# The prologue of a two-layer transformer program: routing by token halves, another order of the loads, Wo summed on TensorE

## The chip, the cores and the metric

One core of one Trainium2 chip runs the whole program. The metric is the device time of one execution in microseconds. TensorE is called PE here, VectorE DVE, ScalarE ACT, GpSimd POOL, and SyncE SP; SP only issues DMA transfers in this program.

## What is computed

2048 tokens of 256 numbers (inputs of shape 2 x 1024 x 256) go through two layers of the form x + s * silu(g), where s is an attention and g a feed-forward part of the same normalized x. The change touches only layer 0:

```python
xn = layernorm(x)
# attention: one K/V head, the values are also the queries of all 16 heads
k, v = xn @ Wk + bk, xn @ Wv + bv
attn = softmax(v @ k.T / 128)                      # per batch
s = concat([attn @ v] * 16) @ Wo + bo              # = (attn @ v) @ sum_over_heads(Wo) + bo
# feed-forward: 64 experts, at most 128 tokens each, hidden size 88
scores = sigmoid(xn @ router_weight.T)
sc = scores + e_bias
# groups of 8 experts, scored by the sum of their two best sc; the 4 best groups stay
masked = where(group in best 4, sc, 0)
topk_idx = top_k(masked, 8)
topk_w = scores[topk_idx] / sum(scores[topk_idx]) * 2.5
# a token's place in an expert = number of earlier tokens that chose it; places over 127 are dropped
moe = scatter_add(silu(x_e @ w_gate[e]) * (x_e @ w_up[e]) @ w_down[e] * topk_w)
g = moe + (silu(xn @ sh_gate) * (xn @ sh_up)) @ sh_down
x = x + s * silu(g)
```

Layer 1 is a grouped attention and a feed-forward part with ternary weights; both kernels compute it by the same code.

## The kernel before

Tokens are in 16 tiles of 128 (NT). Each engine runs a program written out by hand, in order, and semaphores tie them together; there is no scheduler, so the order in the code is the order on the engine. `F` and `A` are two large SBUF areas that several stages use in turn, `two` is the whole of PSUM (eight banks of 128 x 512 float32), W is the area of expert weights and rows.

**Prologue** (to about 85 us). SP loads x in four parts (L311), the router weights and the expert bias (L312, L313), Wk and Wv (L315), their biases (L317), Wo of 2.1 MB (L318) and the weights of the shared expert. DVE takes statistics of x and writes the normalized rows xn (centre, L840). PE waits for the constants and for all six small loads, turns the router weights (L1262), then per tile turns xn into xT (L1279; ACT copies it out of PSUM, L555) and makes the logits of the tile before (L1269, four passes of 64 columns). ACT makes a tanh of them in two halves (L561). K and V follow (L1303, in a buffer of xT's layout `A`), with V turned back to rows (turn_v, L1294). DVE meanwhile routes all 16 tiles at once: scores (L873, L874), the best two of each group by maxima and minima (L877 and on), the four best groups (L892, L896), the masked scores (L899 to L903), the eight best experts (L905, L908), a 0/1 table of experts and tokens (L911) and a running count over it (L912). Then PE turns counts into places (positions, L1338 and L1340), both halves of 32 experts at once, ACT and DVE copy them out (L600, L998), DVE builds the tables by which PE writes each expert's token list (masks L946, hot_high, hot_low, number; slots L1404; spread L982; indices L1413). The normalized weights (L1004 to L1009) are stored beside the rows of xn in DRAM (tok_d, SP, L350). The shared expert is computed between these steps in four groups of 512 tokens: gate and up on PE (shared_up, L1317), tanh on ACT (L587), the product on DVE in two steps (L863, L866), down on PE (L1328), the copy with a factor of 0.25 on ACT (L593). Its rows fill the two DRAM accumulators of the experts' results, acc_d[0] and acc_d[1] (L343; L346 fills rows for tokens that don't exist). POOL writes the constants and adds up Wo over the heads (L428 and L430, 15 additions).

**Expert loop** (64 steps). POOL gathers expert n's rows of tok_d by index (L438), PE turns them (turn, L1432) and makes gate and up (up, L1443), ACT and DVE make the hidden values, PE turns these (turn_h, L1449) and makes down (L1455), DVE scales the rows by the tokens' weights (put, L1023), and POOL scatters them into acc_d[n % 2] with an add (L458). PE's step n is: turn(n+1), up(n), turn_h(n-1), other work, down(n-1). Weights come in groups of two experts in five buffers (load_experts: three transfers a group, L333 and L335). In between stand, by constants: in experts 4 to 7 what is left of the lists of experts 32 to 63 (SLOTS_AT, TURN_AT), and from expert 9 (START) the attention of layer 0 (scores, L1359), whose projection uses WoS, the sum of Wo.

What the names in the change stand for: `rep8`, `gsp`, `gr`, `mx8`, `gmask` are small tables of the group selection; `s_sig`, `s_sc`, `s_masked`, `s_rep` are the scores, biased scores, masked scores and the table with the chosen ones replaced by BIG, all in `F`; `sel16`, `cum16` are the 0/1 table and its count; `then(...)` makes the next DVE instruction wait for this one, `mark(...)` doesn't.

## Time and profile before

| what | value |
|---|---|
| median of three runs | 496.04 us (495.99 to 497.1) |
| the profiled execution | 494.54 us, with a span of 492.7 us |
| mean granted clock of PE over the span | 0.916 |
| busy share over the span | PE 77%, DVE 67%, POOL 64%, PE's weight loads 58%, ACT 46% |
| routing on DVE | 33.50 to 54.6 us |
| first expert's transposes on PE | 85.51 us |
| POOL's eighth scatter (expert 7) | 117.58 us |

The profile is of one execution: the span runs from its first to its last instruction, and its own time holds 1.8 us around that. A share is an average over stages that have different limits, so the table says little by itself; the stages have to be read in time. Starts are counted from the span's start.

### The profile page before, as it was taken

Reading aid. Unit: us, or ns where it says so; the run is one execution under the profiler, and the core shown is the slowest. Engines: PE = TensorE matmul, PEld = TensorE weight load, DVE = VectorE, ACT = ScalarE, POOL = GpSimd, SP = SyncE. Lnnn points to the kernel's source line nnn. Section 1 sums busy time; section 2 is a strip of 40 time slices with the busy share of each in tenths; the row PEclk is TensorE's granted clock in tenths of the full one; section 3 lists DMA queues with packets and bytes.
Section 4 is the critical chain, followed back from the end, with each engine's and each line's share of the span. In section 5 each row is a group of like instructions: output and inputs, shape, how many; then the busy total and the mean of one; then the engine's idle time right before and its main releaser. Section 6 shows DMA issues by size and latency. Waiting matters only on the chain.

```text
span 492.7 us, 7386 instructions
## 1 busy us (share of the span) xinstructions
PE 380.0 (77%) x2246; PEld 286.4 (58%) x2246; DVE 332.1 (67%) x940; ACT 227.7 (46%) x526; POOL 316.9 (64%) x306
## 2 busy tenths in 40 slices
PE   0999868789999878979998973384687857698572
PEld 0974344577776756868886852232365554566562
DVE  6629991855454534646666532859999999999950
ACT  1344323524443436524544423246566656577542
POOL 5440005478887777888888863454787976968872
PEclk9999998799999999979999977589797998889888
DMA  7940056978889997868787546500000000000001
GB/s 251 339 128 0 1 153 220 265 171 196 196 184 226 239 236 172 184 128 204 170 180 171 86 56 195 166 0 0 2 0 23 1 23 1 23 23 11 12 21 43
DMA packets 58872, 57.89 MB, mean 117 GB/s; under 512 B 7099, under 2 KB 56531, under 8 KB 58835
## 3 DMA queue, kind: packets, MB, share of 16 engines
q1 hardware_dynamic: 46547, 38.55, 26.5%
q0 software_dynamic: 12288, 18.88, 20.3%
q8 instruction: 18, 0.29, 0.2%
q14 instruction: 19, 0.16, 0.1%
HBM read 39.69 MB, written 17.73 MB: 117 GB/s over the span
## 4 chain that ended last, share of the span: by engine, by line
DVE 40%; PE 26%; DMA 14%; issue 10%; POOL 4%; ACT 4%; SPq 1%; POOLq 0%; ACTq 0%; DVEq 0%
DMA acc_d<-W,idxE 9%; DVE W L1201 4%; PE two L1395 4%; PE two L1443 4%; DVE nv L1180 3%; DMA W<-tok_d,idxE 3%; PE two L1455 3%; PE two L1359 2%; PE two L1269 2%; DVE nv L1181 2%; DVE W L1204 2%; PE two L1432 2%; DVE W L1023 2%; POOL acc_d L458 2%; PE two L1279 1%
## 5 line engine op out<-in xcount | busy, mean ns | idle before, releaser
L458 POOL DMA_INDIRECT acc_d<-W,idxE x64 | 102.3, 1599 | 28.1 <-issue 13.8
L438 POOL DMA_INDIRECT W<-tok_d,idxE x56 | 56.1, 1002 | 61.6 <-DMA tok_d<-F 44.8
L1046 DVE SCALAR_TENSOR_TENSOR W<-W,two 128x88 f32<-128x88 f32 x64 | 15.6, 244 | 57.8 <-ACT W L678 57.5
L662 ACT ACTIVATE W<-two 128x256 f32<-128x256 f32 x64 | 24.4, 381 | 48.6 <-PE two L1432 48.1
L1543 PE MATMUL two<-wfcT,F 128*128 128x512 f16 x128 | 34.9, 422 | 6.5 <-ACT W L731 6.5
L1395 PE MATMUL two<-A,v 128*128 128x128 f32 x256 | 34.8, 295 | 6.2 <-issue 6.0
L1395 PEld LDWEIGHTS two<-A,v 128*128 128x128 f32 x256 | 33.8, 208 | 8.1 <-issue 7.5
L1023 DVE TENSOR_SCALAR W<-two,W 128x256 f32<-128x256 f32 x56 | 26.8, 479 | 14.7 <-PE two L1455 8.6
L501 POOL TENSOR_TENSOR F<-W,F 128x1024 f16<-128x1024 f32 x16 | 34.1, 2151 | 3.1 <-DVE F L1210 2.6
L1432 PE MATMUL two<-ident,W 128*128 128x128 f32 x112 | 24.3, 300 | 11.4 <-DMA W<-tok_d,idxE 9.2
L1432 PEld LDWEIGHTS two<-ident,W 128*128 128x128 f32 x112 | 19.6, 201 | 22.9 <-DMA W<-tok_d,idxE 13.8
L1443 PE MATMUL two<-W 128*128 128x176 f32 x160 | 32.5, 328 | 0.2 <-ACT W L669 0.2
L1359 PE MATMUL two<-kT,vT 128*128 128x512 f32 x64 | 30.1, 592 | 0.0
L1534 PE MATMUL two<-wqT_hi,F 128*128 128x384 f16 (+1 forms) x64 | 14.4, 329 | 20.2 <-DVE F L1164 20.2
L1583 PE MATMUL two<-wpjT,F 128*128 128x256 f16 x256 | 29.4, 273 | 0.3 <-ACT F L745 0.3
L920 DVE TENSOR_REDUCE nmax<-two 128x1 f32<-128x1024 f32 x16 | 19.6, 1223 | 13.9 <-PE two L1359 13.9
L1583 PEld LDWEIGHTS two<-wpjT,F 128*128 128x128 f16 x256 | 24.9, 98 | 4.3 <-ACT F L745 0.6
L1443 PEld LDWEIGHTS two<-W 128*128 128x128 f32 x160 | 25.9, 204 | 0.7 <-issue 0.7
L1543 PEld LDWEIGHTS two<-wfcT,F 128*128 128x128 f16 x128 | 12.8, 108 | 22.8 <-ACT W L731 8.3
L1455 PE MATMUL two<-W 88*128 88x256 f32 x80 | 24.7, 390 | 1.2 <-DVE W L1023 0.9
L509 POOL TENSOR_TENSOR F<-F 128x256 f32<-128x256 f32 x16 | 11.6, 724 | 21.8 <-DVE F L1217 21.8
L1572 PE MATMUL two<-ident,F 128*128 128x128 f16 x256 | 18.6, 231 | 5.6 <-POOL F L501 3.4
(230 smaller groups left out, 1042.8 us busy)
## 6 DMA issues: line engine op xcount, KB each, us to landing
acc_d<-xn SPq DMA_DIRECT2D x8, 512.0 KB, 4.2
W<-in_L_ffn_w_gate SPq DMA_DIRECT2D x20, 176.0 KB
W<-in_L_ffn_w_up SPq DMA_DIRECT2D x20, 176.0 KB
W<-in_L_ffn_w_down SPq DMA_DIRECT2D x20, 176.0 KB
F<-in_L_ffn_w_gate SPq DMA_DIRECT2D x12, 176.0 KB
F<-in_L_ffn_w_up SPq DMA_DIRECT2D x12, 176.0 KB
F<-in_L_ffn_w_down SPq DMA_DIRECT2D x12, 176.0 KB
x<-in_L_attn_q SPq DMA_DIRECT2D x4, 512.0 KB, 6.0
```

The source lines that it names most:

```text
L438: pool.indirect_dma_start(out=xg[n % XR], out_offset=None, in_=tok_d[:, :], in_offset=bass.IndirectOffsetOnAxis(ap=idxE[:, n:n + 1], axis=0))\
L458: pool.indirect_dma_start(out=acc_d[n % 2][:, :], out_offset=bass.IndirectOffsetOnAxis(ap=idxE[:, n:n + 1], axis=0), in_=ysb[n % YS], in_o ...
L501: pool.tensor_tensor(lo16[n % GT], hid[n // GT % 2][:, n % GT, :], hi16[n % GT], ALU.subtract)\
L662: sc.activation(xgT[n % 2], bk_(2)[:, 0:D].rearrange("p (k n) -> p k n", k=KH), ACT.Copy)\
L1023: ve.tensor_scalar(ysb[n % YS], bk_(3)[:, 0:D], xg[n % XR][:, D + n:D + n + 1], 0.5, ALU.mult, ALU.mult)\
L1359: ins = pe.matmul(two[2][:, 512 * h:512 * h + 512], vT[:, rows], kT[:, at:at + 512], start=True, stop=True)
L1395: ins = pe.matmul(bk_(1)[:, 0:P], v[:, (ORDER[t] // NP) * NP + i, :], probT[t % 2][:, i, :], start=(i == 0), stop=(i == 7))
L1432: ins = pe.transpose(bk_(2)[:, P * k:P * k + P], xg[n % XR][:, 0:D].rearrange("p (n k) -> p k n", k=KH)[:, k, :], ident[:, :])
L1443: ins = pe.matmul(gu[n % 2].rearrange("p (m f) -> p m f", m=2), xgT[n % 2][:, k, :], wgu[r][:, n % WG, :, k, :], start=(k == 0), stop=(k = ...
L1455: pe.matmul(bk_(3)[:, 0:D], hT[n % 2], wdn[(n // WG) % WR][:, n % WG, :], start=True, stop=True)\
L1543: ins = pe.matmul(bk_(2 + h), part[:, n % GT, k, :], wfcT[:, k, 512 * h:512 * h + 512], start=(i == 0), stop=(i == 3))
L1583: ins = pe.matmul(bk_(7)[:, D * (n % GT):D * (n % GT) + D], part[n % 2][:, P * k:P * k + P], wpjT[:, k, :], start=(i == 0), stop=(i == 2 * ...
```

## The change

All of it is in layer 0's prologue and in the first nine experts.

- **Loads and start.** The router weights and the expert bias are first in SP's queue. PE starts with four matmuls on zeros (WARM) whose results nobody reads, then waits for the identity and those two loads alone. DVE makes the zeros, and SP stores them to acc_d[0] and to the rows for tokens that don't exist; only acc_d[1] gets the shared expert's rows, which POOL waits for before expert 1's scatter.
- **Normalizing** is shared: of each four tiles DVE centres two, ACT two (with a bias nmr = -mean * rstd).
- **Routing by halves.** `route(c)` does eight tiles as soon as their logits are there. The sigmoid's factor is folded in (0.5 * tanh + bias + 0.5), groups are masked by a bitwise and, and the scan and the comparison are done for 32 experts at a time (`select(h)`). ACT makes the sigmoid itself from the tanh later.
- **Shared expert.** ACT uses Silu, the product is one DVE step, and the factor of 0.25 is gone. Group 0 of gate and up stands between tile 8 and tile 9 on PE, group 1 ahead of K and V, group 2 after the positions, group 3 after the first indices; down(0) stands between slots and indices, down(2) and down(3) in experts 0 and 1. K and V use two banks instead of four.
- **Wo.** It is loaded into the first half of A, where xT was, once PE has read xT for the last time (`sgu_ps` 4). PE adds it up over the heads by matmuls with the identity, four heads each in experts 3, 6, 7 and 8 (WO_AT); ACT copies the sum in expert 8. POOL's additions are gone.

SP, ahead of the expert loads and after them:

```diff
 ACT_T = 9
+WARM = 4
+WO_AT = (3, 6, 7, 8)
...
         A = sb("A", [P, 8192])
         xT = A[:, 0:4096].rearrange("p (t k n) -> p t k n", t=NT, k=KH)
-        Wo_s = A[:, 4096:8192].rearrange("p (h n) -> p h n", h=HQ)
+        Wo_s = A[:, 0:4096].rearrange("p (h n) -> p h n", h=HQ)
         sh_t = [A[0:FF, 5632 + 512 * i:6144 + 512 * i] for i in range(2)]
-        sh_a = A[0:FF, 6656:7168]
...
         @block.sync
         def _(sp):
+            sp.dma_start(rw_s, rw).then_inc(ld_r, 16)
+            sp.dma_start(eb_b[:, :], eb.rearrange("(a n) -> a n", a=1).to_broadcast([P, NE])).then_inc(ld_r, 16)
             for c in range(4):
                 sp.dma_start(x[:, 4 * c:4 * c + 4, :], x_v[:, 4 * c:4 * c + 4, :]).then_inc(ld_x[c], 16)
-            sp.dma_start(rw_s, rw).then_inc(ld_w0, 16)
-            sp.dma_start(eb_b[:, :], eb.rearrange("(a n) -> a n", a=1).to_broadcast([P, NE])).then_inc(ld_w0, 16)
             for dst, src in ((Wk_s, Wk), (Wv_s, Wv)):
                 sp.dma_start(dst[:, :, :], src.rearrange("(p k) n -> p k n", k=KH)).then_inc(ld_w0, 16)
             for dst, src in ((bkc, bk), (bvc, bv)):
                 sp.dma_start(dst[:, :], src.rearrange("(p a) -> p a", a=1)).then_inc(ld_w0, 16)
-            sp.dma_start(Wo_s, Wo.rearrange("(h p) n -> p h n", p=P)).then_inc(ld_wo, 16)
...
             sp.dma_start(bo_b[:, :], bo.rearrange("(a n) -> a n", a=1).to_broadcast([P, D])).then_inc(ld_sh, 16)
+
+            sp.wait_ge(zeros_ready, 1)
             for c in range(4):
-                sp.wait_ge(xn_ready, 4 * c + 4)
+                sp.dma_start(acc_v[0][:, 4 * c:4 * c + 4, :], zeros.rearrange("p (t d) -> p t d", t=4)).then_inc(acc_zero, 16)
+            for a in acc_d:
+                sp.dma_start(a[NTOK:NTOK + P, :], zeros[:, 0:D]).then_inc(acc_zero, 16)
+            for c in range(4):
+                wait_xn(sp, 4 * c + 1)
+                wait_xn(sp, 4 * c + 3)
                 sp.dma_start(tok_v[:, 4 * c:4 * c + 4, 0:D], xn[:, 4 * c:4 * c + 4, :]).then_inc(xn_stored, 16)
-
-            sp.wait_ge(xn_ready, NT)
...
-                if c == 0:
-                    for a in acc_d:
-                        sp.dma_start(a[NTOK:NTOK + P, :], xn[:, 0, :]).then_inc(acc_init, 16)
-
-            fill_accumulators(0)
             sp.wait_ge(w_ready, 1)
             sp.dma_start(tok_v[:, 0:NT, D:D + NE], s_w).then_inc(w_stored, 16)
             sp.dma_start(tok_d[NTOK:NTOK + P, D:D + NE], s_w[:, 0, :]).then_inc(w_stored, 16)
-            for c in range(1, NT // SC):
-                fill_accumulators(c)
+            for c in range(NT // SC):
+                sp.wait_ge(sy_ready, 2 * c + 2)
+                sp.dma_start(acc_v[1][:, SC * c:SC * c + SC, :], xn[:, SC * c:SC * c + SC, :]).then_inc(acc_shared, 16)
             sp.wait_ge(w_stored, 32)
+            sp.wait_ge(sel_ready, 2)
             for g in range(3, WR):
                 load_experts(g)
+            sp.wait_ge(sgu_ps, 4)
+            sp.dma_start(Wo_s, Wo.rearrange("(h p) n -> p h n", p=P)).then_inc(ld_wo, 16)
             for g in range(WR, NE // WG):
```

POOL, its additions and what it waits for:

```diff
-            pool.wait_ge(ld_wo, 16)
-            then(pool.tensor_tensor(WoS[:, :], Wo_s[:, 0, :], Wo_s[:, 1, :], ALU.add))
-            for h in range(2, HQ):
-                ins = pool.tensor_tensor(WoS[:, :], WoS[:, :], Wo_s[:, h, :], ALU.add)
-                if h < HQ - 1:
-                    then(ins)
-            ins.then_inc(wos_done, 1)
...
-            pool.wait_ge(acc_init, 10 * 16)
+            pool.wait_ge(acc_zero, 6 * 16)
             for n in range(NE):
...
                 pool.wait_ge(y_ready, n + 1)
+                if n == 1:
+                    pool.wait_ge(acc_shared, NT // SC * 16)
```

ACT (the helpers are what the old code did in place, except for `centre` and `sigmoid`):

```diff
+            def centre(c):
+
+                sc.wait_ge(nmr_ready, c + 1)
+                for t in range(4 * c + 2, 4 * c + 4):
+                    sc.activation(xn[:, t, :], x[:, t, :], ACT.Identity, bias=nmr[:, t:t + 1], scale=rstd[:, t:t + 1])\
+                        .then_inc(xn_act, 1)
...
+            def shared_gate(c):
+                sc.wait_ge(sgu_ps, c + 1)
+                if c >= 2:
+                    sc.wait_ge(shT_ready, c - 1)
+                sc.activation(sh_t[c % 2], bk_(shared_bank(c))[0:FF, :], ACT.Silu).then_inc(ssilu_ready, 1)
+
...
+            def sigmoid(c):
+
+                sc.wait_ge(sc_ready, c + 1)
+                sc.activation(s_sig[:, 8 * c:8 * c + 8, :], s_sig[:, 8 * c:8 * c + 8, :], ACT.Copy, bias=0.5, scale=0.5)\
+                    .then_inc(sig_ready, 1)
+
...
             root(0)
             sc.wait_ge(rwT_ps, 1)
             sc.activation(rwT[:, :, :], bk_(4)[:, 0:KH * NE].rearrange("p (k e) -> p k e", k=KH), ACT.Copy).then_inc(rwT_ready, 1)
+            centre(0)
+            take_xT(0)
...
+            take_xT(2)
+            take_xT(3)
+            centre(1)
+            take_xT(4)
+            take_xT(5)
+            root(2)
+            take_xT(6)
+            take_xT(7)
+            centre(2)
+            take_xT(8)
+            root(3)
+            sc.wait_ge(consts, 1)
+            sc.activation(warm[:, :], warm[:, :], ACT.Silu)
+            take_xT(9)
+            take_xT(10)
+            centre(3)
+            take_logits(0)
+            for t in range(11, NT):
+                take_xT(t)
+            take_logits(1)
+            shared_gate(0)
...
+                if n == WO_AT[-1]:
+                    sc.wait_ge(wos_ps, 1)
+                    sc.activation(WoS[:, :], bk_(0)[:, 0:D], ACT.Copy).then_inc(wos_done, 1)
```

DVE:

```diff
+                ve.scalar_tensor_tensor(out=nmr[:, cols], in0=mv[:, cols, 0], scalar=-1.0, in1=rstd[:, cols], op0=ALU.mult,
+                                        op1=ALU.mult).then_inc(nmr_ready, 1)
+                for t in range(4 * c, 4 * c + 2):
                     ve.tensor_scalar(xn[:, t, :], x[:, t, :], mv[:, t, 0:1], rstd[:, t:t + 1], ALU.subtract, ALU.mult)\
-                        .then_inc(xn_ready, 1)
+                        .then_inc(xn_dve, 1)
...
+            ve.wait_ge(ld_r, 2 * 16)
+            then(ve.tensor_scalar(eb_b[:, :], eb_b[:, :], 0.5, None, ALU.add))
             centre(3)
...
 
             def shared_product(c):
-                ve.wait_ge(stanh_ready, c + 1)
-                b = 4 * (c % 2)
-                if c:
-                    ve.wait_ge(shT_ready, c)
-                then(ve.scalar_tensor_tensor(out=sh_a, in0=sh_t[c % 2], scalar=1.0, in1=bk_(b)[0:FF, :], op0=ALU.add, op1=ALU.mult))
+                ve.wait_ge(ssilu_ready, c + 1)
...
+                ve.tensor_tensor(sh_h[c % 2], sh_t[c % 2], bk_(shared_bank(c) + 1)[0:FF, :], ALU.mult).then_inc(shT_ready, 1)
+
+            def route(c):
+
+                ts, gs = slice(8 * c, 8 * c + 8), slice(64 * c, 64 * c + 64)
+                ve.wait_ge(tanh_ready, c + 1)
+                ve.scalar_tensor_tensor(out=s_sc[:, ts, :], in0=s_sig[:, ts, :], scalar=0.5,
+                                        in1=eb_b[:, :].unsqueeze(1).to_broadcast([P, 8, NE]), op0=ALU.mult, op1=ALU.add)\
+                    .then_inc(sc_ready, 1)
+                ve.wait_ge(sc_ready, c + 1)
...
+                then(ve.tensor_scalar(gmask[:, ts, :], gr[:, ts, 0:GROUPS], BIG / 2, -1.0, ALU.is_ge, ALU.mult))
+                then(ve.tensor_tensor(masked_bits[:, gs], sc_bits[:, gs],
+                                      gmask[:, ts, :].rearrange("p t g -> p (t g)").unsqueeze(2)
+                                      .to_broadcast([P, 8 * GROUPS, PER_G]), ALU.bitwise_and))
...
+            def select(h):
+
+                es = slice(HE * h, HE * h + HE)
+                then(ve.tensor_scalar(sel16[:, es, :], s_rep[:, :, es].rearrange("p t e -> p e t"), BIG / 2, None, ALU.is_ge))
+                ve.tensor_tensor_scan(cum16[:, es, :].rearrange("p e t -> p (e t)"), keep16.rearrange("p e t -> p (e t)"),
+                                      sel16[:, es, :].rearrange("p e t -> p (e t)"), 0.0, ALU.mult, ALU.add)\
+                    .then_inc(sel_ready, 1)
+
+            for c in range(2):
+                route(c)
+            select(0)
             shared_product(0)
+            shared_product(1)
...
+            ve.wait_ge(acc_zero, 6 * 16)
             hot_low(0, 0, SB)
             number(0)
 
+            ve.wait_ge(sig_ready, 2)
```

PE:

```diff
-            pe.wait_ge(consts, 1)
-            pe.wait_ge(ld_w0, 6 * 16)
+            pe.wait_ge(zeros_ready, 1)
+            for _ in range(WARM):
+                pe.matmul(bk_(7), zeros[:, 0:P], zeros[:, 0:512], start=True, stop=True)
+            pe.wait_ge(ident_ready, 1)
+            pe.wait_ge(ld_r, 2 * 16)
...
+            def shared_up(c):
+                if c == 0:
+                    pe.wait_ge(ld_sh, 4 * 16)
+                    pe.wait_ge(xT_ready, SC)
+                if c >= 2:
+                    pe.wait_ge(shT_ready, c - 1)
+                for m in range(2):
...
+                if t == NT // 2:
+                    shared_up(0)
...
+            shared_up(1)
+            pe.wait_ge(ld_w0, 4 * 16)
...
+            positions(0)
+            shared_up(2)
             pe.wait_ge(v_ready, 4)
...
+            def sum_wo(i):
+
+                if i == 0:
+                    pe.wait_ge(ld_wo, 16)
+                    pe.wait_ge(sy_ready, NT // 2)
+                for h in range(4 * i, 4 * i + 4):
+                    ins = pe.matmul(bk_(0)[:, 0:D], ident[:, :], Wo_s[:, h, :], start=(h == 0), stop=(h == HQ - 1))
+                if i == 3:
+                    ins.then_inc(wos_ps, 1)
+
             pe.wait_ge(pos_act, 1)
             for g in range(HG):
                 slots(0, g)
+            shared_down(0)
             indices(0)
+            shared_up(3)
+            positions(1)
             shared_down(1)
-            shared_up(3)
-            shared_down(2)
-            shared_down(3)
...
-            pe.wait_ge(sy_ready, NT // 2)
+            pe.wait_ge(sy_ready, 4)
             pe.wait_ge(idxE_ready, 1)
+            pe.wait_ge(pos_act, 2)
...
+                if n < 2:
+                    shared_down(2 + n)
+                if n in WO_AT:
```

**Where instructions stand now.** `two` is PSUM, W and A are the areas above; the words in brackets are the semaphores that an instruction waits for. First PE in expert 3, before:

```order
L1443 MATMUL two<-W 128x176 [waits hT_ready,ld_e1,xgT_ready]
L1443 MATMUL two<-W 128x176
L1449 MATMUL two<-ident,W 88x128 [waits h_ready]
L1455 MATMUL two<-W 128x256 [waits y_ready,hT_ready]
L1432 MATMUL two<-ident,W 128x128 [waits xgT_ready,xg_ld5]
```

and after:

```order
L1525 MATMUL two<-W 128x176 [waits hT_ready,ld_e1,xgT_ready]
L1525 MATMUL two<-W 128x176
L1531 MATMUL two<-ident,W 88x128 [waits h_ready]
L1495 MATMUL two<-A,ident 128x256 [waits sy_ready,ld_wo]
L1495 MATMUL two<-A,ident 128x256 x3
L1537 MATMUL two<-W 128x256 [waits y_ready,hT_ready]
L1514 MATMUL two<-ident,W 128x128 [waits xgT_ready,xg_ld5]
```

Between turning the hidden values of expert 2 and its down matmul, PE now adds up four heads of Wo, and waits there for its load (ld_wo). SP's queue from the routing weights on, before:

```order
L343 DMA acc_d<-xn 128x4x256 [waits sy_ready]
L343 DMA acc_d<-xn 128x4x256
L346 DMA acc_d<-xn 128x256 x2
L350 DMA tok_d<-F 128x16x64 [waits w_ready]
L351 DMA tok_d<-F 128x64
L343 DMA acc_d<-xn 128x4x256 [waits sy_ready]
L343 DMA acc_d<-xn 128x4x256
L343 DMA acc_d<-xn 128x4x256 [waits sy_ready]
L343 DMA acc_d<-xn 128x4x256
L343 DMA acc_d<-xn 128x4x256 [waits sy_ready]
L343 DMA acc_d<-xn 128x4x256
L333 DMA F<-in_L_ffn_w_gate 128x2x176 [waits w_stored]
```

and after:

```order
L366 DMA tok_d<-F 128x16x64 [waits w_ready]
L367 DMA tok_d<-F 128x64
L370 DMA acc_d<-xn 128x4x256 [waits sy_ready] x4
L358 DMA F<-in_L_ffn_w_gate 128x2x176 [waits sel_ready,w_stored]
L358 DMA F<-in_L_ffn_w_up 128x2x176
L360 DMA F<-in_L_ffn_w_down 88x2x256
L358 DMA F<-in_L_ffn_w_gate 128x2x176
L358 DMA F<-in_L_ffn_w_up 128x2x176
L360 DMA F<-in_L_ffn_w_down 88x2x256
L376 DMA A<-in_L_attn_Wo 128x16x256 [waits sgu_ps]
L358 DMA W<-in_L_ffn_w_gate 128x2x176 [waits y_ps]
```

The fills of shared rows now stand behind the store of the weights and go to one accumulator, and Wo's load stands behind these fills and two groups of expert loads. Last, ACT around the logits, before:

```order
L547 ACTIVATE rstd<-rstd 128x4 [waits ln1_var]
L555 ACTIVATE A<-two 128x256 [waits xT_ps] x12
L561 ACT_TABLE_LOAD
L561 ACTIVATE F<-two 128x512 [waits logits_ps] x2
L573 ACTIVATE kT<-two,bks 128x512 [waits kv_ps,bks_ready]
```

and after:

```order
L573 ACTIVATE A<-two 128x256 [waits xT_ps]
L562 ACTIVATE rstd<-rstd 128x4 [waits ln1_var]
L630 ACT_TABLE_LOAD
L630 ACTIVATE warm<-warm 128x1 [waits consts]
L573 ACTIVATE A<-two 128x256 [waits xT_ps] x2
L568 ACTIVATE xn<-x,nmr,rstd 128x256 [waits nmr_ready]
L568 ACTIVATE xn<-x,nmr,rstd 128x256
L578 ACTIVATE F<-two 128x512 [waits logits_ps]
L573 ACTIVATE A<-two 128x256 [waits xT_ps] x5
L578 ACTIVATE F<-two 128x512 [waits logits_ps]
L590 ACTIVATE A<-two 88x512 [waits sgu_ps]
```

The first half's tanh (L578) now stands among the tiles, behind two tiles and two centred rows that come after tile 8, and the table load stands ahead of them.

## Rows read from the trace of the kernel before

**Rows 1.** Page, busy time and shares of the span.
```profile
PE 380.0 (77%) x2246; PEld 286.4 (58%) x2246; DVE 332.1 (67%) x940; ACT 227.7 (46%) x526; POOL 316.9 (64%) x306
```

**Rows 2.** Chain of waits in the prologue: start us, us, what.
```profile
5.83 6.32 DMA bvc<-in_L_attn_bv
...
16.15 0.43 PE two L1279 x2
...
17.32 0.43 PE two L1279 x2
...
33.50 0.70 DVE F L873
```

**Rows 3.** Timeline, weight loads and matmuls: start us, us, engine, line, what [idle before].
```profile
33.01 0.34 PEld L1303 LDWEIGHTS two<-A,F 128*128 128x128 f32 x1 [0.52 <-issue]
...
33.86 0.34 PEld L1303 LDWEIGHTS two<-A,F 128*128 128x128 f32 x1 [0.52 <-issue]
...
34.48 0.19 PEld L1303 LDWEIGHTS two<-A,F 128*128 128x128 f32 x1 [0.28 <-issue]
34.91 0.19 PEld L1303 LDWEIGHTS two<-A,F 128*128 128x128 f32 x1 [0.24 <-issue]
...
50.18 3.64 PE L1317 MATMUL two<-A,sgu 128*88 128x512 f32 x8 [0.78 <-ACT v L566]
```

**Rows 4.** Windows: stretch, length, PE, PEld, DVE, ACT, POOL, PE clock, DMA share, GB/s.
```profile
19.00:20.00 1.00, 1.00 (x8) 1.00 (x7) 1.00 (x2) 0.34 (x1) 0.92 (x2) 1.00 1.09 385
92.00:93.00 1.00, 0.20 (x1) 0.23 (x2) 0.88 (x5) 1.00 (x5) 0.97 (x1) 0.62 1.03 270
297.00:298.00 1.00, 0.91 (x7) 0.45 (x5) 0.00 (x0) 0.85 (x3) 0.00 (x0) 0.98 0.77 84
```

**Rows 5.** Groups by line and form, DVE, prologue: busy us, mean ns, idle before.
```profile
L908 DVE MATCH_REPLACE8 F<-mx,F 128x64 f32<-128x64 f32 x16 | 3.1, 205 | 0.0
L912 DVE TENSOR_TENSOR_SCAN F<-F 128x1024 f16<-128x1024 f16 x1 | 2.3, 2291 | 0.0
...
L874 DVE TENSOR_TENSOR F<-F,eb_b 128x1024 f32<-128x1024 f32 x1 | 1.2, 1226 | 0.0
...
L982 DVE TENSOR_TENSOR F<-two,diag 128x512 f32<-128x512 f32 x1 | 0.7, 692 | 0.0
```

**Rows 6.** Timeline, from the positions to the first expert.
```profile
54.67 0.39 PE L1338 MATMUL two<-F,before 128*128 128x512 f16 x1 [0.85 <-DVE F L912]
...
56.67 0.29 DVE L946 TENSOR_SCALAR F<-F 128x512 int16<-128x512 int16 x1
...
85.51 0.50 PE L1432 MATMUL two<-ident,W 128*128 128x128 f32 x2 [0.69 <-ACT xn L593]
```

**Rows 7.** Timeline, POOL: first gather, second and eighth scatter.
```profile
74.92 1.20 POOL L438 DMA_INDIRECT W<-tok_d,idxE  x1 [44.84 <-DMA tok_d<-F]
...
97.26 1.59 POOL L458 DMA_INDIRECT acc_d<-W,idxE  x1 [0.30 <-issue]
...
117.58 1.59 POOL L458 DMA_INDIRECT acc_d<-W,idxE  x1 [0.30 <-DVE W L1023]
```

**Rows 8.** Timeline, SP's queue issues, and POOL's first reader of Wo.
```profile
6.46 0.60 SPq L318 DMA_DIRECT2D A<-in_L_attn_Wo  x1
...
18.10 0.72 POOL L428 TENSOR_TENSOR WoS<-A 128x256 f32<-128x256 f32 x1 [7.30 <-DMA A<-in_L_attn_Wo]
...
95.74 0.37 SPq L333 DMA_DIRECT2D W<-in_L_ffn_w_gate  x1
...
96.69 0.42 SPq L335 DMA_DIRECT2D W<-in_L_ffn_w_down  x1
```

**Rows 9.** Timeline, PE and DVE in experts 3 to 9.
```profile
94.65 1.06 PE L1455 MATMUL two<-W 88*128 88x256 f32 x2
...
109.85 1.88 PE L1359 MATMUL two<-kT,vT 128*128 128x512 f32 x4
...
115.11 0.48 DVE L1023 TENSOR_SCALAR W<-two,F 128x256 f32<-128x256 f32 x1
```

270 lines of the change are left out of this document (128 added, 142 removed).

## The prediction

> **What bounds the kernel now.** I read the page's shares first: no engine is full over the whole span (PE 77%, DVE 67%, POOL 64%) [rows 1], so the bound has to be read by stage. The expert loop is paced by POOL: scatters start 3.19 us apart (97.26 to 117.58 holds the second to the eighth, one longer step among them; the scatter's own issue takes 1.59 of a step, a gather's issue and the gaps the rest) [rows 7]. What starts the loop later starts all that follows later, and POOL has almost nothing to catch up with. So the change is worth what it moves the eighth scatter (expert 7, 117.58), the first one by which all changed work is done. Ahead of the loop I read the chain of waits, then each engine's timeline: PE waits for the last bias until 12.15, then turns tiles and makes logits; DVE routes from 33.50 [rows 2] until PE takes the positions at 54.67 [rows 6]; slots, indices and the shared expert follow, and the first expert's transposes start at 85.51 [rows 6].
>
> **PE's start, clock and logits.** PE no longer waits for six small loads but for two, router weights and bias, which are first in the queue. The x loads start 1.24 us later for it (two small issues). Two sets of statistics, the reciprocal and two rows lie between x and the first rows: about 10.0 instead of 12.7. Then the clock decides. Before, one tile (two transposes, four logits passes) takes 1.17 us (16.15 to 17.32, and so for the tiles after it), and a transpose 0.21 of it (two take 0.43) [rows 2]; these are times of the lower level, since in the later, dense K/V work a half matmul goes from 0.85 us (33.01 to 33.86) to 0.43 (34.48 to 34.91) [rows 3]. The granted clock shows 1.00 there only because its first change is not yet recorded. The four warm-up matmuls are eight halves of 0.85, 6.8 us at most, done by 8.5. They may raise the clock. After them PE has 1.5 to 3 us of nearly nothing, then tiles that come as DVE delivers them, at about half use. In the loop the clock fell within 92 to 93, where PE worked 0.20 us of one [rows 4]. So I take the lower level again from about the third tile: tile 8 at 18.5, its predecessor's logits at 19.7.
>
> Here speaks a row against me: at 297 the clock rose to 0.98 while PE did nothing but transposes [rows 4]. If transposes keep it up as well as they raise it, the logits stage could run at the upper level; that is the second rival. The Trainium skill ("TensorE: Matmul & The Clock Gate", Part 4, PE-mode transpose) says the opposite, that transposes do not count as activity for the gate. By it the stage would stay low, as I forecast; the row contradicts it as a reason.
>
> **Shared gate matmuls in the middle.** The first group (eight halves, 3.64 us at the upper level [rows 3]) now stands between tile 8 and tile 9. Starting low it costs between 3.4 (it rises at once) and 6.9 (never); in the K/V work it rose near 34.3 [rows 3], some way in, so I take the middle, 5.1: 24.8. ACT turns to the first half's tanh only after two more tiles and two rows that it now centres, all behind that group: 27.7. The new table load for Silu stands where ACT waits for PE, and the one for Exp ahead of a wait: both nothing, 1.3 each if uncovered.
>
> **Routing by halves.** The chain before is 21.1 us from 33.50 to 54.6 [rows 2, 6]. A half has eight of each per-tile instruction (16 replaces at 0.205 [rows 5]), and half-wide elementwise ones: 0.69 instead of 1.23 [rows 5]. One TENSOR_SCALAR of 0.70 and the one for sigmoid go. I get 9.3 per half, 18.7 for both, and half of the compare and the scan (2.29 [rows 5]), 1.8. From 27.7 that is 48.2, 6.4 earlier. But PE stands behind it: from 24.8, seven tiles at 0.6 plus ACT's tanh (30.9), the second gate group (3.4), then K and V (32 halves of 0.43, 13.8), 16 turns at half of 0.21 (1.7) and 0.6 of waits for ACT's last evacuations: 50.4. PE is 2.2 us later than DVE, so positions go from 54.67 to 50.4. Half of what routing gains is covered by PE.
>
> **From positions to the first expert.** Before this takes 30.84 us (54.67 to 85.51). Now the tables of 32 experts go first, ACT evacuates them (2.0 instead of 1.3 until DVE starts masks, 56.67 before [rows 6]), DVE's seven microseconds are the same, but PE idles 4.8 us before the slots and starts them low (32 instructions, half as long again). The weights w leave SP without two accumulator fills ahead, so gathers can start some 18 us after the positions; before it was 20.3 (54.67 to 74.92 [rows 6, 7]). Of the shared expert only one gate group (the last) and down(0), down(1) stay between slots and loop: gate 2 runs while PE waits for masks, down(2) and down(3) in experts 0 and 1. Added up from the positions: 2.0 to the masks, 6.9 to the end of numbering (DVE), slots 5.7, down(0) and indices 2.2, gate group 3.5, positions of the second half 0.5, down(1) with its evacuation 2.8: 23.6. The first gather would be there at about 22.5, so PE decides. First expert: 74.0, **11.5 us earlier** than 85.51 [rows 6].
>
> **Wo is asked for before it is there.** This pays it back. Wo's load can't start before the gate groups have read xT, and in SP's queue it stands behind the four fills of shared rows (the last waits for the evacuation in expert 1, 7.5 us after the first expert) and behind six expert loads (three issues take 1.4 us [rows 8], and the fill's own 0.6): issued 11.1 us after the first expert. Before, it took 11.6 us from issue (6.46) to landing (18.10), behind what was left of x and the small weights [rows 8]; now a megabyte of expert weights and a fill are ahead of it. So it lands 22.5 us after the first expert, at 96.5. PE asks for it in expert 3, about 10.5 us after the first. It stands for 12 us (bounds: 8, if its 2.1 MB move from the issue on at the best rate of 385 GB/s [rows 4] and land 2 us later, and 14), and behind it are down(1), so expert 1's rows and POOL's second scatter.
>
> After landing: four sums of Wo at the lower level 3.4, down(1) 0.9, then what PE did before from 94.65 to 109.85 (down(1) to the first scores, 15.2 us [rows 9], of which 2.4 were waits that are now covered and 0.5 is down(1) itself), plus the three other sums at 1.7: 22 us to the scores. Before, the last put ahead of the eighth scatter starts 5.3 us after the scores (109.85 to 115.11 [rows 9]) and ends half a us later; then it had 2 us of room, now it is the limit. 96.5 + 22 + 5.8 = 124.3 less some tenths that overlap: 124, against 117.58.
>
> **Sum.** Eighth scatter +6 us; the loop and the second layer follow unchanged. POOL loses its 15 additions, which nobody waited for. On the profiled execution, 494.54 us with a span of 492.7, this gives 500.5; that execution lies 1.5 us below the median of the three runs, 496.04, on which it gives **502 us**.
>
> **Rivals.**
> 1. *As above*, 499 to 505. Chance 0.50.
> 2. *The clock holds through the logits* (by the rows of rising with transposes [rows 4]). Tiles are then limited by DVE (3.45 us per four), gate group 3.4, positions at 46.5, first expert at 70.1, Wo at 92.6: eighth scatter +2, **498 us** (496 to 500). For it: PE warmed just ahead. Against: the gap and the half use. Chance 0.20.
> 3. *Faster: Wo is in time, or nearly.* One mechanism: the stall in expert 3. The earlier start (11.5) is kept if Wo lands within 16.5 us of the first expert; below that the kernel is faster. With no stall PE still has 6.9 us of sums and 3.8 of down groups more, less 5 that the loop's start waits for DVE: −6 us, **490 us** (489 to 494). For it: nothing else reads much then, and POOL idles. Against: 2 MB alone need 5.5 us at 385 GB/s, after an issue at 11.1. Chance 0.17.
> 4. *Slower still*: the clock also stays low in experts 4 to 8 (as within 92 to 93 [rows 4]) and each sum costs 3.4: +11, **507 us**. Chance 0.08. The rest, 0.05, is spread to both sides.
>
> The range takes rivals 1, 2 and 4 with their bounds and leaves out 3: 495 to 507.5. A difference of 0.3% (1.5 us) is what a measurement can tell from no change. Faster by more: 0.17 + 0.02 + 0.02 = 0.21. Within: about a third of rival 2, and edges: 0.12. Slower: 0.67.
>
> **What would show it.** Right: PE's warm-up from about 1.6; the first tile near 10 and 1.17 us per tile; positions at 50 and not before DVE's scan ends; first expert's transposes at 74; a PE wait of about 12 us for the DMA of A (Wo) in expert 3, with POOL idle before its second scatter; 3.19 us steps again from the eighth scatter at 124. Wrong: a tile pace of 0.6 us (rival 2); Wo landing less than 16.5 us after the first expert (rival 3); gathers after 98 held by anything but PE's results.

## The result, and the profile after

The changed kernel takes 505.04 us in the median of four runs (501.43 to 507.16), against 496.01 (four runs, 495.43 to 497.1) for the kernel before: a ratio of 1.0172, with a 95% interval of 1.0109 to 1.0235. The forecast was 502. The profiled execution took 507.16 us, the slowest of the four, against 494.54 before.

The page says nothing by its shares, as before [rows 1]:

```profile
PE 382.6 (76%) x2286; PEld 285.7 (57%) x2286; DVE 324.7 (64%) x948; ACT 233.2 (46%) x540; POOL 307.9 (61%) x291
```

PE's timeline of the changed kernel (start us, us, engine, line, what, idle before) has the whole story:

```profile
2.04 5.39 PE L1328 MATMUL two<-F 128*128 128x512 f32 x8 [2.04 <-DVE F L891]
...
11.89 1.08 PE L1372 MATMUL two<-ident,xn 128*128 128x128 f32 x4 [4.09 <-DVE xn L901]
...
15.04 0.64 PE L1372 MATMUL two<-ident,xn 128*128 128x128 f32 x2
...
16.22 0.63 PE L1372 MATMUL two<-ident,xn 128*128 128x128 f32 x2
...
22.09 5.54 PE L1352 MATMUL two<-A,sgu 128*88 128x512 f32 x8
27.46 0.39 PE L1372 MATMUL two<-ident,xn 128*128 128x128 f32 x2
...
28.09 0.44 PE L1372 MATMUL two<-ident,xn 128*128 128x128 f32 x2
...
53.54 0.38 PE L1414 MATMUL two<-F,before 128*128 128x512 f16 x1
...
62.47 5.80 PE L1476 MATMUL two<-F 128*128 128x256 f16 x32 [4.91 <-DVE F L1031]
...
76.80 0.50 PE L1514 MATMUL two<-ident,W 128*128 128x128 f32 x2 [0.69 <-issue]
...
101.51 3.43 PE L1495 MATMUL two<-A,ident 128*128 128x256 f32 x8 [13.34 <-DMA A<-in_L_attn_Wo]
...
122.19 1.88 PE L1431 MATMUL two<-kT,vT 128*128 128x512 f32 x4
```

DVE's timeline has the landing of x's first part and the end of the first half's scan, 2.2 us ahead of the positions:

```profile
7.91 1.41 DVE L907 BATCH_NORM_STATS2 st<-x 128x6 f32<-128x256 f32 x4 [5.93 <-DMA x<-in_L_attn_q]
...
50.17 1.22 DVE L974 TENSOR_TENSOR_SCAN F<-F 128x512 f16<-128x512 f16 x1
```

The first expert starts at 76.80, where it was 85.51 [rows 6]: 8.7 us earlier. Then PE stands still for 13.34 us in expert 3 until Wo lands, and the first scores start at 122.19, where they were at 109.85 [rows 9]. POOL's timeline shows what that does to the scatters (the rows are the first, second and eighth; the second and eighth were at 97.26 and 117.58 [rows 7]), and SP's queue shows why Wo is late:

```profile
88.15 1.65 POOL L473 DMA_INDIRECT acc_d<-W,idxE  x1 [6.15 <-DMA acc_d<-xn]
...
106.18 1.59 POOL L473 DMA_INDIRECT acc_d<-W,idxE  x1 [15.08 <-DVE W L1090]
...
128.21 1.59 POOL L473 DMA_INDIRECT acc_d<-W,idxE  x1 [1.96 <-DVE W L1090]
```

```profile
66.59 0.37 SPq L366 DMA_DIRECT2D tok_d<-F  x1
67.00 1.29 SPq L367 DMA_DIRECT2D tok_d<-F  x1
70.67 14.66 SPq L370 DMA_DIRECT2D acc_d<-xn  x4
85.42 0.45 SPq L358 DMA_DIRECT2D F<-in_L_ffn_w_gate  x1
...
88.84 0.37 SPq L376 DMA_DIRECT2D A<-in_L_attn_Wo  x1
```

PE had read xT for the last time near 74, when the fourth gate group (70.31, 3.65 us) ended. The four fills kept the queue until 85.3 and six expert loads until 88.8. (The first of the three POOL rows names a fill as what ended the wait; nothing in the program makes that scatter wait for one. DVE's rows of expert 0 end at 87.87, and that is what it had to wait for.)

The eighth scatter comes 10.6 us later than before, and the profiled execution takes 12.6 us more. From the eighth scatter to the end it is 379.0 us here and 377.0 before; in the twelve versions below this part takes 375.5 to 380.8 whatever was changed ahead of it. So the remaining 2 us are no more than single executions differ by, and I assign them to nothing. The +10.6 is to be held against the median's +9.0 us.

### The profile page after: what moved, and what is told of

It is laid out like the page before. It is cut to its first block, busy times and chain, and to the rows that moved or that the text cites. A ratio compares the mean times of both kernels' runs of the same rounds, so it can differ in the third digit from the quotient of the medians.

```text
span 505.3 us, 7480 instructions
## 1 busy us (share of the span) xinstructions
PE 382.6 (76%) x2286; PEld 285.7 (57%) x2286; DVE 324.7 (64%) x948; ACT 233.2 (46%) x540; POOL 307.9 (61%) x291
## 4 chain that ended last, share of the span: by engine, by line
PE 33%; DVE 30%; DMA 13%; issue 11%; POOL 7%; ACT 3%; SPq 1%; another core or an unknown queue 0%; POOLq 0%; ACTq 0%; DVEq 0%
DMA acc_d<-W,idxE 6%; DVE W L1268 4%; PE two L1525 4%; DVE nv L1247 3%; DMA W<-tok_d,idxE 3%; PE two L1467 3%; PE two L1431 3%; PE two L1537 3%; POOL acc_d L473 3%; PE two L1402 3%; DMA A<-in_L_attn_Wo 2%; PE two L1352 2%; DVE nv L1248 2%; PE two L1514 2%; PE two L1476 2%
## 5 line engine op out<-in xcount | busy, mean ns | idle before, releaser
L451 POOL DMA_INDIRECT W<-tok_d,idxE x56 | 57.9, 1033 | 78.3 <-DVE idxE L1060 61.5
L1632 PE MATMUL two<-wfcT,F 128*128 128x512 f16 x128 | 36.1, 432 | 6.7 <-ACT W L787 6.7
L1514 PE MATMUL two<-ident,W 128*128 128x128 f32 x112 | 23.7, 293 | 13.3 <-DMA W<-tok_d,idxE 9.9
L1525 PE MATMUL two<-W 128*128 128x176 f32 x160 | 31.2, 318 | 0.0
L1525 PEld LDWEIGHTS two<-W 128*128 128x128 f32 x160 | 24.8, 196 | 0.4 <-issue 0.4
L524 POOL TENSOR_TENSOR F<-F 128x256 f32<-128x256 f32 x16 | 11.6, 726 | 21.8 <-DVE F L1284 21.8
L787 ACT ACTIVATE W<-two,fcscale 128x1024 f32<-128x1024 f32 x16 | 17.8, 1114 | 12.1 <-issue 8.1
```

The lines of the kernel that those rows point to most:

```text
L451: pool.indirect_dma_start(out=xg[n % XR], out_offset=None, in_=tok_d[:, :], in_offset=bass.IndirectOffsetOnAxis(ap=idxE[:, n:n + 1], axis=0))\
L1514: ins = pe.transpose(bk_(2)[:, P * k:P * k + P], xg[n % XR][:, 0:D].rearrange("p (n k) -> p k n", k=KH)[:, k, :], ident[:, :])
L1525: ins = pe.matmul(gu[n % 2].rearrange("p (m f) -> p m f", m=2), xgT[n % 2][:, k, :], wgu[r][:, n % WG, :, k, :], start=(k == 0), stop=(k = ...
L1632: ins = pe.matmul(bk_(2 + h), part[:, n % GT, k, :], wfcT[:, k, 512 * h:512 * h + 512], start=(i == 0), stop=(i == 3))
```

## Experiments

Every version is compared with the kernel before, run on the same chip. "Base" is what it was made from. The chips differ a little: the kernel before had medians of 496.4 us beside e1 to e4, 496.9 beside e5 to e8, 498.5 beside e9 to e11 and 497.3 beside e12. Versions of different groups are therefore to be compared by their ratios.

| version | base | median us | ratio to before (interval) | positions | first expert | eighth scatter |
|---|---|---|---|---|---|---|
| before | | 496.0 | 1 | 54.67 | 85.51 | 117.58 |
| changed kernel | | 505.0 | 1.0172 (1.0109 to 1.0235) | 53.54 | 76.80 | 128.21 |
| e1: Wo asked for earlier | changed | 491.5 | 0.9922 (0.9882 to 0.9962) | 51.76 | 74.55 | 111.22 |
| e2: sums in experts 7, 8 | changed | 492.7 | 0.9938 (0.9912 to 0.9965) | 53.67 | 76.84 | 117.02 |
| e3: Wo on POOL | changed | 488.0 | 0.9827 (0.9786 to 0.9867) | 52.42 | 75.20 | 109.13 |
| e4: gate group 0 behind the logits | changed | 505.9 | 1.0201 (1.0166 to 1.0236) | 55.17 | 77.77 | 128.23 |
| e5: no warm-up | e3 | 488.8 | 0.9820 (0.9747 to 0.9894) | 52.51 | 75.24 | 108.97 |
| e6: x first | e3 | 483.6 | 0.9722 (0.9646 to 0.9799) | 48.82 | 70.10 | 103.92 |
| e7: early tanh | e3 | 488.7 | 0.9796 (0.9714 to 0.9878) | 52.46 | 75.73 | 110.68 |
| e8: early tanh, gate group 1 late | e3 | 482.5 | 0.9674 (0.9597 to 0.9750) | 50.19 | 71.64 | 106.39 |
| e9: e6 and e8 together | e3 | 485.0 | 0.9731 (0.9670 to 0.9792) | 50.14 | 71.60 | 106.80 |
| e10: e6 without warm-up | e6 | 487.5 | 0.9793 (0.9721 to 0.9866) | 51.92 | 74.58 | 109.49 |
| e11: e9's edits, but e1's Wo | e1 | 488.9 | 0.9808 (0.9737 to 0.9880) | 47.08 | 69.33 | 111.01 |
| e12: x whole and first, five warm-ups | e9 | 485.7 | 0.9746 (0.9711 to 0.9781) | 49.70 | 71.15 | 106.76 |

Positions, first expert and eighth scatter are starts in the one profiled execution of each version; the medians are of four to eleven runs.

### Is it the wait for Wo?

**e1.** Wo's load is moved in SP's queue:

```diff
@@ SP
+            sp.wait_ge(sgu_ps, 4)
+            sp.dma_start(Wo_s, Wo.rearrange("(h p) n -> p h n", p=P)).then_inc(ld_wo, 16)
             for c in range(NT // SC):
                 sp.wait_ge(sy_ready, 2 * c + 2)
...
-            sp.wait_ge(sgu_ps, 4)
-            sp.dma_start(Wo_s, Wo.rearrange("(h p) n -> p h n", p=P)).then_inc(ld_wo, 16)
```

> The changed kernel with one thing moved: in SP's queue the load of Wo stands right behind the store of the routing weights, ahead of the four fills of shared rows and of two groups of expert weights. If PE's wait in expert 3 (13.3 us in the trace of the changed kernel) is what makes it slow, Wo is issued near 74 and lands by about 86, ahead of expert 3 at 88; the wait is gone, the eighth scatter goes from 128.2 to 111 to 115 (before: 117.6), and the time from 505 to 490 to 494. Rival: the loss sits in what PE does more in the loop (sums and shared expert); then the time stays above 500 with the wait gone. Second rival: 2 MB earlier hold up gathers and fills; then the first scatter moves from 88 to beyond 92 and the time is about 497.

**e2.** The load stays, the sums move: `WO_AT = (7, 8)`, eight heads each.

> The changed kernel with the sums of Wo in experts 7 and 8, eight heads each, instead of 3, 6, 7 and 8; the load stays where it is. If the wait is a matter of place alone, Wo lands 24.7 us after the first expert as it does now and PE asks for it some 24.5 us after: a wait under 1.5 us, the eighth scatter at 113 to 116, and 491 to 495 us. Rival (more work in the loop is the loss): above 500. Rival (the wait moves along with the sums, because the load is late for a reason in the loop): a wait over 5 us in expert 7.

**e3.** Wo goes back to where the kernel before has it; PE's sums and ACT's copy are gone, and ACT waits for POOL's sum before it writes over that memory:

```diff
-        Wo_s = A[:, 0:4096].rearrange("p (h n) -> p h n", h=HQ)
+        Wo_s = A[:, 4096:8192].rearrange("p (h n) -> p h n", h=HQ)
...
             sp.dma_start(bo_b[:, :], bo.rearrange("(a n) -> a n", a=1).to_broadcast([P, D])).then_inc(ld_sh, 16)
+            sp.dma_start(Wo_s, Wo.rearrange("(h p) n -> p h n", p=P)).then_inc(ld_wo, 16)
...
+            pool.wait_ge(ld_wo, 16)
+            then(pool.tensor_tensor(WoS[:, :], Wo_s[:, 0, :], Wo_s[:, 1, :], ALU.add))
+            for h in range(2, HQ):
...
             take_logits(1)
+            sc.wait_ge(wos_done, 1)
             shared_gate(0)
```

> The changed kernel with Wo handled as in the kernel before: loaded in the prologue (behind the other small loads), added up on POOL, no sums in the loop. If the prologue's gain is real and only Wo took it back, the first expert stays near 77, POOL paces the loop from the first scatter near 88 on in steps of 3.19, the eighth scatter stands near 110.5 to 113, and the time is 487 to 491 us. Rival (the earlier start is worth nothing because the loop is bound elsewhere): 495 to 497. Rival (POOL's additions slow DVE's routing): the first expert after 79 and 491 to 494.

All three took the loss away, each in another way. In e1 the load is issued at 71.73 (SP), and PE's sums in expert 3 follow without a wait (PE):

```profile
71.73 0.37 SPq L369 DMA_DIRECT2D A<-in_L_attn_Wo  x1
72.15 11.32 SPq L372 DMA_DIRECT2D acc_d<-xn  x4
```

```profile
86.04 0.27 PE L1531 MATMUL two<-ident,W 128*88 128x128 f32 x1
86.15 1.89 PE L1495 MATMUL two<-A,ident 128*128 128x256 f32 x8
```

The sums themselves now take 1.89 us at a granted clock of 1.00, where behind the standstill they took 3.43 at 0.55. e1 landed at 491.5 (490 to 494 was expected here, and 489 to 494 in the prediction's third rival). Its first scatter starts at 86.31, so the second rival, gathers and fills held up beyond 92, did not come, though the second expert's rows were waited for a little (1.38 us). In e2 the same load, still late, costs 1.56 us, because PE asks for it only when it is nearly there:

```profile
102.04 3.72 PE L1495 MATMUL two<-A,ident 128*128 128x256 f32 x16 [1.56 <-DMA A<-in_L_attn_Wo]
```

492.7 was expected; its eighth scatter, 117.02, came later than the 113 to 116 that I gave. e3, with nothing of Wo left on PE in the loop, is at 488.0 and its eighth scatter 8.5 us ahead of the kernel before, 19.1 ahead of the changed one; the profiled executions differ by 6.6 and 19.2. So the wait in expert 3 turned a gain of some 4 us (e1, e2) into a loss of 9. PE's sums together with a load among the gathers cost another 3.5 us against POOL's additions in the prologue (e1 against e3, whose intervals do not overlap); no run separates these two. That more work in the loop as such is the loss, the rival, falls: e1 and e2 have all of it.

### What holds the prologue?

**e4.** Gate group 0 moves from between tile 8 and 9 to behind the last logits (`shared_up(0)` after `logits(NT - 1)`).

> The changed kernel with the first group of the shared expert's gate and up moved from between tile 8 and 9 to behind the last logits. If that group is what raises TensorE's clock for the tiles behind it (0.7 us a tile there, 1.17 ahead of it), all tiles now take 1.17 us, the logits end near 31 instead of 34, but the group still follows at 5.5, so K and V start about 2.5 us later, the positions at 56, the first expert at 79.4, and the time is 507 to 508; DVE starts the first half of the routing some 5 us earlier and has to wait for PE. Rival (DVE, not PE, holds the positions): they come 3 to 5 us earlier and the time is 500 to 502.

All sixteen tiles now took 1.17 us and the granted clock stayed at 0.50 from 14 to 28 us, so the group is what raised the clock for the tiles behind it. The price was smaller than expected, since groups 0 and 1, now in one piece, took 7.87 us together and not 9.1: positions 1.6 us later, the first expert 1.0, and 505.9 us, no measurable difference from 505.0.

**e5, e6.** On the base of e3: `WARM = 0`; and the first part of x ahead of the two small loads:

```diff
+            sp.dma_start(x[:, 0:4, :], x_v[:, 0:4, :]).then_inc(ld_x[0], 16)
             sp.dma_start(rw_s, rw).then_inc(ld_r, 16)
             sp.dma_start(eb_b[:, :], eb.rearrange("(a n) -> a n", a=1).to_broadcast([P, NE])).then_inc(ld_r, 16)
-            for c in range(4):
+            for c in range(1, 4):
```

> The version with Wo on POOL (e3) without the four warm-up matmuls. In its trace the first eight tiles take 1.17 us each as in the kernel before, though the warm-up ran until 8; if the warm-up is worth nothing, the tiles, the first expert (75.2) and the time (488.0) stay within 1 us. Rival: the warm-up is what lets the first gate group rise early (4.6 us here, up to 6.9 if it stayed low); then the first expert comes 1 to 2.3 us later, 489 to 490.5.

> The version with Wo on POOL with the first part of x ahead of the router weights in SP's queue. In the trace of the changed kernel DVE waits for x until 7.9, 3.6 us longer than in the kernel before (4.3), where x was first. If the two small loads cost that, the first tile comes near 9.7 instead of 11.9, the first expert 1.5 to 2.4 us earlier, 486 us. Rival: the router weights or the bias now land last and PE waits for them: first tile at 11 or later, and 488.

Without the warm-up nothing moved: first expert 75.24 instead of 75.20. With x first the first tile came 2.2 us earlier than in e3 (9.45 against 11.62) and the first expert 5.1. In time the step is less sure: the intervals of e6 and e3 still touch. PE's timeline of e6:

```profile
2.04 6.17 PE L1334 MATMUL two<-F 128*128 128x512 f32 x8 [2.04 <-DVE F L897]
8.13 0.45 PE L1338 MATMUL two<-ident,F 64*128 64x64 f32 x2
9.45 0.90 PE L1378 MATMUL two<-ident,xn 128*128 128x128 f32 x4 [0.86 <-DVE xn L907]
...
11.01 0.44 PE L1378 MATMUL two<-ident,xn 128*128 128x128 f32 x2
...
11.68 0.44 PE L1378 MATMUL two<-ident,xn 128*128 128x128 f32 x2
...
16.41 3.62 PE L1358 MATMUL two<-A,sgu 128*88 128x512 f32 x8
...
48.82 0.61 PE L1420 MATMUL two<-F,before 128*128 128x512 f16 x1 [2.56 <-DVE F L980]
```

A tile takes 0.67 us from the first on (9.45 is the start of two tiles) and the gate group 3.62: these are the durations of the upper level (2.4 GHz), where all other versions show those of 1.2 GHz in their first eight tiles (1.17 us). The granted clock of the changed kernel agrees, 0.57 in 12 to 14 and 0.50 in 14 to 16. In e6 it reads 1.00 there, but by itself this would prove little: in e10, below, it reads 1.00 too at 1.17 us a tile. The warm-up is the same; the pause behind it and the turned router weights is 0.86 us and not 3 or 4. The weight loads of the warm-up show that it does reach the upper level (steps of 0.85 us between halves, then 0.43), at about 5.4 in the changed kernel, first, and at 7.1 in e6:

```profile
4.76 0.33 PEld L1328 LDWEIGHTS two<-F 128*128 128x128 f32 x1 [0.52 <-issue]
5.54 0.19 PEld L1328 LDWEIGHTS two<-F 128*128 128x128 f32 x1 [0.45 <-issue]
5.97 0.19 PEld L1328 LDWEIGHTS two<-F 128*128 128x128 f32 x1 [0.24 <-issue]
```

```profile
6.46 0.34 PEld L1334 LDWEIGHTS two<-F 128*128 128x128 f32 x1 [0.52 <-issue]
7.18 0.19 PEld L1334 LDWEIGHTS two<-F 128*128 128x128 f32 x1 [0.38 <-issue]
```

In the one it was lost again as the tiles began, in the other kept. That the rise came late in e6 is not what kept it: in e3 and e8 it came as late (at about 7.0), the pauses were 3.16 and 3.42 us, and the tiles took 1.17. The short pause itself is not owed to the order of the loads alone. In e6, e9, e10 and e11 SP issues x and the two small loads in the same order, and the second part of x, which the first tile needs too, landed at 7.39, 9.67, 8.54 and 8.76. The profiled execution of e6 had the luck of the earliest landing, and how many of its four runs kept the clock isn't known.

**e10** asks whether the warm-up does it: e6 with `WARM = 0`.

> The version with x first and Wo on POOL (e6), without the four warm-up matmuls. In e6 the tiles went at 0.67 us from the first one on and PE had stood still only 0.9 us between the warm-up and the first tile; in the other versions it had stood still 3.2 to 4.1 us and they went at 1.17. If the warm-up with a short pause behind it is what keeps the clock up, the first eight tiles take 1.17 us without it, the first gate group 4.5 to 5.5 us instead of 3.6, the first expert comes near 72.5 to 73.5 instead of 70.1, and the time is 485 to 487 instead of 483.6. Rival (the clock in e6 has another cause, the x load and its earlier start): tiles stay at 0.67 and 483.6.

The tiles are back at 1.17 us, the gate group at 4.99, the first expert at 74.58 and the time at 487.5. The first expert came 4.5 us later, one us more than expected, but 1.15 us of it is the second part of x, which landed later in that execution (8.54, against 7.39). So in these two traces the warm-up was worth some 3 us with a short pause behind it, where with a long one it was worth nothing (e5). The medians don't settle it: the ratios are 0.972 and 0.979, and their intervals overlap.

**e7, e8.** On the base of e3: ACT's tanh of the first half ahead of tiles 9 and 10 and its two centred rows; then also gate group 1 behind the positions:

```diff
             sc.activation(warm[:, :], warm[:, :], ACT.Silu)
+            take_logits(0)
             take_xT(9)
             take_xT(10)
             centre(3)
-            take_logits(0)
...
-            shared_up(1)
             pe.wait_ge(ld_w0, 4 * 16)
...
             positions(0)
+            shared_up(1)
             shared_up(2)
```

> The version with Wo on POOL, with ACT's tanh of the first half ahead of tiles 9 and 10 and the two rows that it centres, instead of behind them. DVE then starts routing at about 24.5 instead of 30.4. If PE holds the positions (the step of the prediction), they stay near 52.4, PE waits for nothing more or less, and the time stays at 488, within 1 us. Rival (DVE is what holds them): positions 3 to 5 us earlier and 483 to 485.

> As the run with the early tanh, and also the second gate group of the shared expert moved from ahead of K and V to behind the positions, where PE idled 4.9 us. If PE was the bound up to the positions and DVE now has its result by 47, they come 3.4 us earlier, at 49, the group is covered by the idle time, the first expert comes at 72 and the time is 484 to 485. Rival (each of the two is only half of the bound, or ACT's order takes it back): 487 to 488.

In e7 DVE starts routing at 24.01 instead of 29.32, and the positions stay where they are, 52.46 for 52.42: PE holds them. In e8 the group is out of PE's way, and they come at 50.19, now waiting for DVE, whose scan ends at 50.14; the first expert comes at 71.64, and the time is 482.5 (484 to 485 was expected):

```profile
50.19 0.39 PE L1418 MATMUL two<-F,before 128*128 128x512 f16 x1 [1.37 <-DVE F L979]
```

That the positions were not at 49 has a cause that I had not foreseen. DVE's timeline, first of the changed kernel, then of e7, the same instructions:

```profile
30.44 0.69 DVE L931 SCALAR_TENSOR_TENSOR F<-F,eb_b 128x512 f32<-128x512 f32 x1 [7.17 <-ACT F L578]
31.16 0.42 DVE L938 TENSOR_TENSOR F<-F 128x256 f32<-128x256 f32 x1
...
33.54 0.22 DVE L947 TENSOR_TENSOR F<-F 128x64 f32<-128x64 f32 x1
33.80 0.22 DVE L950 TENSOR_TENSOR gsp<-F 128x64 f32<-128x64 f32 x1
34.06 0.65 DVE L953 MAX8 mx<-gsp 128x8 f32<-128x8 f32 x8
```

```profile
24.01 1.15 DVE L936 SCALAR_TENSOR_TENSOR F<-F,eb_b 128x512 f32<-128x512 f32 x1
25.20 0.83 DVE L943 TENSOR_TENSOR F<-F 128x256 f32<-128x256 f32 x1
...
30.96 0.77 DVE L952 TENSOR_TENSOR F<-F 128x64 f32<-128x64 f32 x1
31.77 0.77 DVE L955 TENSOR_TENSOR gsp<-F 128x64 f32<-128x64 f32 x1
32.57 0.64 DVE L958 MAX8 mx<-gsp 128x8 f32<-128x8 f32 x8
```

POOL adds up Wo meanwhile, in e7 from 20.55 to 33.26, and most of DVE's sums and maxima of two tensors take some 0.4 to 0.6 us longer, for instance 0.77 where they took 0.22 (two of the eleven that start between 25.2 and 31.8 kept their old length). The MAX8, which reads one tensor, is not touched. POOL's own additions go on at 0.85 us a piece (11.90 us for 14). Five us of head start are two when both halves are done. In e6, whose positions wait 2.56 us for DVE, the same additions lie beside the routing.

**e9, e11, e12** put the edits together.

> All four edits that helped or were meant to: Wo on POOL, x first, the early tanh and the second gate group behind the positions. If PE and DVE both hold the positions and each edit takes from one of them, positions near 45 to 46, the first expert near 67 to 68, time 479 to 481. POOL's additions run beside the first half of the routing, whose sums of two tensors took 0.75 us instead of 0.22 to 0.29 there in e7; this costs DVE 4 us at that place. Rival (DVE, slowed by POOL, holds the positions): positions at 47 to 48 as in e6, first expert at 69 to 70, time 482 to 484.

> The same as the version with all edits, but with Wo summed on PE in the loop and its load ahead of the fills (as in e1). POOL no longer hinders DVE in the prologue, so positions near 43 to 45 and the first expert near 65 to 67; in the loop four sums cost PE what they cost in e1 (eighth scatter 36.7 us after the first expert there, 33.9 in e3). If these two cancel, time 478 to 482, level with the version on POOL. Rival (Wo's load is late again, since the whole start moved 8 us and the last reader of xT with it less): a wait in expert 3 over 3 us and 484.

> As the version with all edits and Wo on POOL (e9), but all four parts of x go ahead of the router weights in SP's queue, as in the kernel before, and there are five warm-up matmuls. In e9 the second part of x landed at 9.67, since the two small loads stood between it and the first; DVE makes its statistics ahead of centring the first tiles, so the first tile came at 11.7, PE stood still 2.9 us behind the warm-up, and the tiles went at 1.17 us. With x whole and first, the second part is there at 6.3 as in the kernel before, the first tile comes at 9.0 to 9.5, the pause is under 1 us, and if a short pause is what keeps the clock (0.9 us did in e6, 1.6 us did not in e11), the tiles take 0.67 us, the second half's tanh comes 5 us earlier than in e9, the positions at 44 to 46, the first expert at 66 to 68, and the time is 479 to 481. Rival (the router weights now land last and PE waits for them behind the warm-up): a pause over 1.5 us, tiles at 1.17, and 484 to 486.

None came to 480, so all three expectations failed. Each trace shows where the time went. In e9 (485.0) the second part of x landed at 9.67; DVE makes its statistics ahead of centring the first tiles, so the pause behind the warm-up was 2.86 us and the tiles went at 1.17. In e12 (485.7) the rival that I had named came true: x was there at 6.21, but the expert bias landed last, and PE waits for it with the router weights:

```profile
2.04 6.55 PE L1333 MATMUL two<-F 128*128 128x512 f32 x10 [2.04 <-DVE F L896]
11.02 0.42 PE L1337 MATMUL two<-ident,F 64*128 64x64 f32 x2 [2.44 <-DMA eb_b<-in_L_ffn_e_bias]
```

In e11 (488.9) the prologue was the shortest of all, with the positions at 47.08 and the first expert at 69.33, and POOL left DVE alone: the first half of the routing took 9.54 us, where it takes 14.55 in e9, which differs only in where Wo is loaded and added up. The gain was given back at once. PE's timeline of e11:

```profile
69.33 0.48 PE L1515 MATMUL two<-ident,W 128*128 128x128 f32 x2 [0.92 <-DMA W<-tok_d,idxE]
73.89 0.70 PE L1515 MATMUL two<-ident,W 128*128 128x128 f32 x2 [4.08 <-DMA W<-tok_d,idxE]
...
75.56 3.62 PE L1364 MATMUL two<-sdn,A 88*128 88x256 f32 x8
```

The second expert's rows, gathered from 66.93 on, were not there until 73.9. Wo's 2 MB had been issued at 66.28, between the two first gathers; I take it that they held the gather up (in e1, where Wo was issued 1.94 us after the first gather's start, the second expert still waited 1.38 us for its rows; in e3, without Wo, none). Behind the pause the first down group of the shared expert takes 3.62 us at a granted clock of 0.50, instead of 1.89. From first expert to eighth scatter e11 takes 41.7 us, e1 36.7, e3 33.9.

The lowest ratio is e8's (0.9674, 482.5 us), then come e6, e9 and e12; all are 2 to 4% faster than the kernel before. The intervals of the four overlap, and which is the best one is open.

## Why the prediction was right

The sign, the mechanism and its place were right: an earlier first expert, then a wait of PE for Wo in expert 3 that costs more. Point by point:

- **x and the first tile: mis-sized.** x landed at 7.91 and not 5.5, and the first tile came at 11.89, not 10.0. I had charged the two small loads with their issue (1.24 us), not with the time that their transfers take from x; and DVE's statistics of the second part of x stand ahead of the first tile's centring, so that part counts too (e6, e9). Of the 3.6 us by which x landed later than before, the issues explain 1.24; how the transfers share the rest was not measured.
- **Clock: right here, by a condition I had only half named.** Tiles took 1.17 us with the warm-up before them. e6 shows the second rival's mechanism at work: with a pause of 0.86 us the clock held through the logits. That its first expert came at 70.1, the very number of that rival's sum, is luck: e6 is another kernel (x first, Wo on POOL), its positions came at 48.8 and not 46.5, and from there to the first expert it took 21.3 us and not 23.6. What I had set against the rival were the pause and PE's half use once the tiles come. The half use never came: in the changed kernel PE is busy for all of 12 to 16 us. On transposes the runs say little: in e6 they came mixed with logits.
- **Gate group in the middle:** 5.54 us for 5.1; routing 20.95 us (30.44 to 51.39) for 20.5; positions 2.2 us behind DVE, as forecast (e7 confirms that PE held them); from the positions to the first expert 23.3 us for 23.6. So the late start went through: 1.9 us at the first tile, 2.7 when the gate group was done, 2.8 at the first expert.
- **Wo:** issued 12.0 us after the first expert (11.1), landed 24.7 after it (22.5): its transfer took 12.6 us, a little more than the 11.6 between issue and first reader before [rows 8]. PE asked for it 11.4 us after the first expert (10.5) and stood 13.3 us for 12.
- **From landing to scores** 20.7 us for 22, then 6.0 to the eighth scatter (5.8): 128.2 for 124.3. Of the 3.9 us, 2.8 are the late start and 2.2 the landing, less 1.1 here. So the forecast of +6 us was too small at the eighth scatter (+10.6) and in the median (+9.0), by the size of terms and not by their kind.
- **"The loop and the second layer follow unchanged"** is right within the 2 us by which that part differs between executions.
- **Rivals:** Wo in time would have given 490; e1 gave 491.5. The low clock in experts 4 to 8 did not come: later sums took 1.89 us. The later sums were costed at 1.7 each, and start 1.73 us ahead of what follows them.
